# The lo parts of the shared expert's up weights: a subtraction moved from GpSimd to VectorE

## What is computed

```python
x = layernorm(hidden)                                  # 2048 x 512
scores = sigmoid(x @ gate_w)                           # 32 experts in 4 groups
# the 2 best groups, of them the 6 best experts, weights normalised
shared = (silu(x @ sw_gate) * (x @ sw_up)) @ sw_down   # 512 -> 704 -> 512, all tokens
out = hidden + shared + sum(weight * expert(x))        # 6 experts per token
```

## Time and profile before

| what | us |
|---|---|
| median of 3 runs | 3377.06 |
| lowest, highest of them | 3371.04, 3385.72 |
| the profiled execution, its own time | 3374.1 |
| its span in the trace | 3372.4 |
| mean granted TensorE clock, share of full speed | 0.958 |

### The profile page before, as it was taken

How to read it: one execution, slowest core, us unless ns; L and a number is a source line. 1 busy time by engine, 2 the same in 40 slices (tenths; PEclk the granted TensorE clock), 3 DMA queues, 4 the chain that set the end, 5 groups by cost and what they waited for, 6 DMA issues and landing times. The chain is left out here.

```text
span 3372.4 us, 62799 instructions
## 1 busy us (share of the span) xinstructions
PE 3143.9 (93%) x15962; PEld 2452.9 (73%) x15965; DVE 2083.4 (62%) x3584; ACT 1592.0 (47%) x2095; POOL 904.2 (27%) x772
## 2 busy tenths in 40 slices
PE   7989999999799899999999968878998999999996
PEld 6745555555577699999899933335787999999996
DVE  4266666663585466666666649987654666666664
ACT  2224444444321256665556656634123656656663
POOL 0011000110111233333333314432012444443332
PEclk9969999999899999999999978988998999999998
DMA  5331111130310367776776540114115777777664
GB/s 178 114 72 39 39 40 39 40 101 1 118 32 22 109 168 174 177 169 168 170 180 166 116 134 0 50 63 147 40 40 155 178 180 183 170 181 168 176 138 111
DMA packets 141339, 383.49 MB, mean 114 GB/s; under 512 B 22112, under 2 KB 22880, under 8 KB 137568
## 3 DMA queue, kind: packets, MB, share of 16 engines
q1 hardware_dynamic: 87456, 252.66, 23.7%
q0 software_dynamic: 52608, 127.69, 20.3%
q10 hardware_dynamic: 1152, 1.57, 0.2%
HBM read 281.42 MB, written 104.63 MB: 114 GB/s over the span
## 5 line engine op out<-in xcount | busy, mean ns | idle before, releaser
L1728 DVE TENSOR_TENSOR first_lo<-first_raw,first_hi x232 | 562.7, 2426 | 121.3 <-ACT first_hi L1671 121.3
L1625 POOL DMA_INDIRECT acc_rows<-g_y,first_ids_out x232 | 377.3, 1626 | 902.2 <-ACT g_y L1682 712.1
L594 DVE TENSOR_REDUCE b_part_max<-b_p_ring 128x1 f32<-128x512 f32 (+3 forms) x640 | 359.9, 606 | 229.3 <-PE b_p_ring L681 142.1
L1671 ACT ACTIVATE first_hi<-first_raw x232 | 469.6, 2024 | 48.3 <-DMA first_raw<-in_expert_weights_dram 33.1
L568 ACT ACTIVATE b_probs<-b_p_cols 128x1024 f32<-128x1024 f32 (+1 forms) x320 | 269.3, 893 | 320.9 <-PE b_p_cols L699 320.9
L1721 DVE TENSOR_TENSOR g_hidden<-g_gate,g_p_up 128x352 f32<-128x352 f32 x232 | 120.9, 521 | 446.8 <-PE g_p_up L1788 446.4
L1786 PE MATMUL g_p_gate<-first_hi,g_rows_hi 128*128 x928 | 321.8, 347 | 6.5 <-DVE first_lo L1728 6.5
L1682 ACT ACTIVATE g_y<-g_p_y,first_rows_in 128x512 f32<-128x512 f32 x232 | 159.6, 688 | 329.6 <-PE g_p_y L1804 329.5
L1787 PE MATMUL g_p_gate<-first_lo,g_rows_hi 128*128 x928 | 303.0, 327 | 0.0
L1788 PE MATMUL g_p_gate<-first_hi,g_rows_lo 128*128 x928 | 301.6, 325 | 0.0
L1786 PE MATMUL g_p_up<-first_hi,g_rows_hi 128*128 x928 | 297.9, 321 | 0.0
(11 more groups left out here) (326 smaller groups left out, 6479.1 us busy)
## 6 DMA issues: line engine op xcount, KB each, us to landing
first_raw<-in_expert_weights_dram SPq DMA_DIRECT2D x248, 544.0 KB
acc_rows<-f_acc SPq DMA_DIRECT2D x34, 256.0 KB, 2.0
qk_hi<-a_hi SPq DMA_DIRECT2D x32, 256.0 KB, 2.6
qk_lo<-a_lo SPq DMA_DIRECT2D x32, 256.0 KB, 2.9
xn_rows<-f_xn SPq DMA_DIRECT2D x8, 1024.0 KB, 5.2
b_q_stack<-qk_hi SPq DMA_DIRECT2D x28, 256.0 KB
b_k_stack<-qk_hi SPq DMA_DIRECT2D x28, 256.0 KB
first_raw<-in_expert_weights_dram SPq DMA_DIRECT2D x2, 2176.0 KB, 8.8
```

Source lines behind the costliest of these rows:

```text
L594: v.tensor_reduce(part_max[:, h, t % BT, c:c + 1], p_ring[:, ring, 0:w], AX.X, ALU.max).then_inc(rows_free, 1)
L1625: pool.indirect_dma_start(out=acc_rows, out_offset=bass.IndirectOffsetOnAxis(ap=ids_out[:, i:i + 1].bitcast(U32), axis=0), in_=y[:, n, :], ...
L1671: act.activation(hi[:, bass.ds(place, PIECE)], raw[:, bass.ds(source, PIECE)], ACT.Copy).then_inc(split_hi_ready, 1)
L1728: v.tensor_tensor(lo[:, bass.ds(place, PIECE)], raw[:, bass.ds(source, PIECE)], hi[:, bass.ds(place, PIECE)].bitcast(F32), ALU.subtract).t ...
```

## The change

GpSimd's two subtractions are taken out of its list. The same two instructions, with the same waits for `up_hi_ready` and the same count of `up_lo_ready`, stand in VectorE's list, behind the normalisation of the last block and ahead of `low_rows(0)` (the `xT_lo` of the first block).

```diff
@@ GpSimd's list
                 pool.affine_select(out=before_b[:], in_=zeros_b[:], ...).then_inc(consts, 1)
 
-                for i in range(2):
-                    pool.wait_ge(up_hi_ready, i + 1)
-                    pool.tensor_tensor(wup_lo[:, :, UP_HALF[i]], wup[i][:], wup_hi[:, :, UP_HALF[i]].bitcast(F32), ALU.subtract).then_inc(up_lo_ready, 1)
-
                 for i in range(NB):
@@ VectorE's list
                     for t in range(BT):
                         norm.vector_normalize(v, b, t, xn[:, b % 2 * BT + t, :], resid[:, place_of(b) + t, :]).then_inc(normed, 1)
+                for i in range(2):
+                    v.wait_ge(up_hi_ready, i + 1)
+                    v.tensor_tensor(wup_lo[:, :, UP_HALF[i]], wup[i][:], wup_hi[:, :, UP_HALF[i]].bitcast(F32), ALU.subtract).then_inc(up_lo_ready, 1)
                 low_rows(0)
                 v.wait_ge(down_hi_ready, 2)
```

## The result

The changed kernel takes 3358.47 us (median of 6 runs, 3356.20 to 3371.08) against 3374.05 us (median of 6, 3368.34 to 3389.25): 15.6 us less, a ratio of 0.9959 with a 95% interval of 0.9942 to 0.9977. The forecast was 15.3 us less, a ratio of 0.9955, or 3361.7 us counted from the 3377.06 us that the kernel before then had as its median. Timed again later with 10 runs beside 17 of the kernel before, the ratio was 0.9956 (0.9943 to 0.9970).

A forecast was written before the change was run, and what follows sets the result against it. TensorE was taken to bound the kernel; 7.66 and 7.68 us gained in the two routers, with VectorE's work and the down load costing nothing, made 3377.06 - 15.3 = 3361.7 us, range 3354 to 3370.

The forecast's parts named there:

- The blocking: Before block 2, GpSimd's subtractions hold up normalisations; without them block 2 starts 5.95 and 4.93 us sooner in the routers.
- Rival (c): Long normalisations come from a coincidence of stores and normalisations, not GpSimd, and stay; gain 0, 3377 us; chance 0.05.
- The clock: Without the standstill block 2 takes 5.81 us, not 7.52 and 8.57, so turn(0) starts 7.66 and 7.68 us sooner.
- Rival (a): The low clock stays in block 2 of both routers: 10.9 us gained, 3366.2 us; chance 0.22.
- rival (b): A 4.70 us clock dip in the second router's first large matmuls vanishes: 17 to 18 us gained, 3359.5; chance 0.15.
- VectorE's work: Two subtractions behind block 3's normalisations take 6.2 us per router, hidden in VectorE's idling before xT_lo; cost nothing.
- The down load: The down weights' load leaves 3.7 us later, takes about 6.5 us, with 5 us of slack at ScalarE; costs nothing.
- Rival (d): The down load reaches ScalarE late, leaving behind VectorE's half 0: 4.7 us lost per router, 3386 us; chance 0.03.
- The sum: From turn(0) on the shift is carried to the end: 7.66 + 7.68 = 15.3 us gained, 3361.7 us.

The follow-up runs named there:

- the filler: The kernel before, with 42 transposes of the identity on TensorE in the standstill ahead of block 2; 3363.9 us, executed once.
- gpsimd_behind: The kernel before, with both subtractions kept on GpSimd but waiting for the last normalisation; 3361.27 us, ratio 0.9942 to the kernel before.
- statistics_again: The changed kernel with block 1's statistics made ahead of those of blocks 2 and 3, timed again; 3353.68 us, ratio 0.9946 to the kernel before.
- two passes: The changed kernel with VectorE's two subtractions made twice; 3363.6 us, executed once.
- three passes: The changed kernel with VectorE's two subtractions made three times; 3374.15 us, ratio 1.0008 to the kernel before.

## Why the prediction was right

*The blocking.* Right. Both of GpSimd's subtractions each held one normalisation; without GpSimd at that place all are 0.54 us, with one half back one long one is back, and with GpSimd later the gain is the same within the intervals. Rival (c), a coincidence, fell. What the text left out is how little one blocking costs: 0.8 us of path for the first alone.

*The clock.* Right in size and side: I took the upper end, 7.66 and 7.68 us; 7.77 and 7.81 were measured at `turn(0)`, and the filler shows 1.67 and 2.71 us of the 1.71 and 2.77 that block 2's length had promised. In the second router the closeness is partly luck: the sum took block 1 as fixed, and its length by the clock varies by 1.2 us between traces (8.55 us of work before, 8.30 and 8.61 in the two traces of the changed kernel, 7.44 in gpsimd_behind). Rival (a), the low clock kept, did not occur in either trace of the changed kernel (block 2 in 5.81 us in all four routers), but it did once in statistics_again, where block 2 of the second router, after a standstill of 3.06 us, took 7.44 us. Of rival (b), the reason was wrong. The dip did stay away in the changed kernel:

```profile
2303.40:2308.10 4.70, 4.70 (x20) 3.83 (x21) 3.12 (x2) 1.54 (x2) 0.00 (x0) 1.00 0.67 235
```

But in the kernel before, the second router, with the dip, needs 90.32 - 51.18 = 39.14 us between the two marks, and the first, without it, 83.93 - 44.75 = 39.18. The dip cost nothing there, so its absence could give nothing: where TensorE is not slowed, it stands 1.22 us for VectorE's `h` in the middle of turning the next block (1.33 in the changed kernel), and that wait takes up the dip.

*VectorE's work.* Right: 6.09 us for the estimated 6.2, hidden; two passes still fit.

*The down load.* Right that it costs nothing here, wrong in its slack. It left 27.35 us behind the router's start; with the 8.3 us that it takes when the stores follow it, it was in, by this estimate, about 4 us ahead of ScalarE's reading in the first router and 2.7 us in the second (2291.09 + 8.3 against 2302.09), not 5. Rival (d) is therefore nearer than I priced it: its mechanism is right (lateness at ScalarE is lost almost one for one, as two and three passes show), but a further 2.7 us of delay already reaches it, and three passes made the kernel as slow as before by it.

*The sum.* 15.3 forecast, 15.6 measured, and 15.57 at the second marks. Counted from each router's first GpSimd instruction to the first matmul of the experts behind it, the changed kernel is 8.6 and 9.1 us shorter in its first trace and 7.3 and 8.6 in its second (280.14 and 287.24 us before; 271.52 and 278.19, 272.81 and 278.68 after): the shift arrives whole, give or take 1.3 us. It is not TensorE alone that carries it, as the prediction had it, since TensorE waits for VectorE's `h` once on the way; VectorE's list has shifted by the same amount.

## To carry to other kernels

An instruction that is blocked by another engine looks busy, not idle: a group whose longest member is many times its median (here 6.94 beside 0.54 us), ending just behind an instruction of the other engine, is the sign. Moving GpSimd's instruction in time cured it as well as moving it to another engine; what to watch is what was queued behind the moved one, here a load of some 8.3 us from issue to landing with about 3 to 4 us to spare.

## What else the runs showed

- Expected, and now with numbers: VectorE's subtraction with both inputs in SBUF and GpSimd's exclude each other (begun 0.02 us later, GpSimd's took 8.81 us instead of 5.6), and a GpSimd fill, which reads nothing, holds a normalisation (2.96 us for 0.54).
- Not expected: the load of 1.4 MB took 8.1 to 8.5 us from issue to ScalarE's start, wherever ScalarE waited for it; in all of these two stores of 1 MB were issued right behind it on the same queue. In the kernel before, without them, it was some 6.5 us by the estimate of the prediction. That the stores cause the difference was not tested by a run of its own.
- Not expected: the rest of the kernel scatters in single executions by as much as this change is worth. In twelve traces the time from the second mark of the first router to the start of the second router was 1298.2 to 1308.0 us, and from the second router's second mark to the end 1013.4 to 1028.6 us, with no relation to the edit. Most of it lies in the two expert stages: from the first matmul of the experts to the first matmul of the stage behind them it is 809.5 to 817.5 us, and from that of the second router's experts to the end 816.5 to 831.1 us, while the stage between the first experts and the second router takes 291.6 to 294.3 us from its first matmul on. What causes this stayed open, no run was made for it. It is why a single execution says nothing here about 4 us.
